# A three-phase transformer kernel on one core: the loop of phase B written out, a division and a scale step moved in phase A, weight rounding and half of the output products moved in phase B, and the residual add split between ScalarE and GpSimd

## What is computed

```python
x = x + attn_a(layernorm(x))     # 1024 tokens x 512, 32 heads of 16, full softmax, biases
x = x + ffn(layernorm(x))        # base product + routed low-rank experts, top 2 of 8
x = x + attn_b(layernorm(x))     # 32 heads of 128, 8 key/value groups
x = x + ffn(layernorm(x))        # the same weights again

def attn_b(h):                   # 4-bit weights with a scale for each 128 rows
    w = (qw - 8) * repeat(scales, 128)
    q, k, v = h @ w_q, h @ w_k, h @ w_v;  q, k = rope(q), rope(k)
    p = softmax(where(causal, q @ k.T / sqrt(128), min))
    return (p @ v) @ w_o
```

## Time and profile before

| | |
|---|---|
| median of 3 runs | 1618.2 us (1615.97 to 1626.73) |
| the profiled execution | 1621.11 us, of it 1619.3 us span |
| TensorE busy | 1480.0 us (91%) |
| VectorE busy | 1239.5 us (77%) |
| ScalarE busy | 868.7 us (54%) |
| GpSimd busy | 237.6 us (15%) |
| chain that ended last | PE 71%, DVE 12%, issue 6%, ACT 4%, DMA 4% |

### The profile page before, as it was taken

How to read it: one execution, slowest core, us unless ns; L and a number is a source line. 1 busy time by engine, 2 the same in 40 slices (tenths; PEclk the granted TensorE clock), 3 DMA queues, 4 the chain that set the end, 5 groups by cost and what they waited for, 6 DMA issues and landing times.

```text
span 1619.3 us, 25526 instructions
## 1 busy us (share of the span) xinstructions
PE 1480.0 (91%) x7932; PEld 700.4 (43%) x7932; DVE 1239.5 (77%) x2583; ACT 868.7 (54%) x1468; POOL 237.6 (15%) x174
## 2 busy tenths in 40 slices
PE   5789999999998998899998988998988999999979
PEld 3412323233332354455554544554544544555534
DVE  4288888888886378787897877897877886877863
ACT  2205767666766423565565554674654664655631
POOL 2102000000000042211212211212212221211020
PEclk8958999999999999899999999999999999999999
DMA  3993000000000323467576566675675674653631
GB/s 94 153 141 120 1 1 0 0 0 0 0 0 0 72 79 104 98 131 144 124 136 132 125 119 129 135 142 117 127 134 115 130 156 98 136 103 63 104 66 52
DMA packets 352266, 144.96 MB, mean 90 GB/s; under 512 B 314680, under 2 KB 324408, under 8 KB 352128
## 3 DMA queue, kind: packets, MB, share of 16 engines
q1 hardware_dynamic: 352144, 143.48, 42.9%
HBM read 59.64 MB, written 6.19 MB: 41 GB/s over the span
## 4 chain that ended last, share of the span: by engine, by line
PE 71%; DVE 12%; issue 6%; ACT 4%; DMA 4%; SPq 2%; ACTq 0%; DVEq 0%; POOL 0%
PE ps L1444 9%; PE ps L1446 9%; PE ps L1445 9%; PE ps L1226 9%; PE ps L1279 7%; PE ps L1265 6%; PE ps L1406 3%; PE ps L1525 3%; PE ps L1527 3%; PE ps L1526 3%; DMA hlT<-hl 2%; DVE mx L834 2%; SPq L470 2%; PE ps L1369 2%; DMA scratch<-pieces 2%
## 5 line engine op out<-in xcount | busy, mean ns | idle before, releaser
L834 DVE TENSOR_REDUCE mx<-ps 128x1 f32<-128x512 f32 x512 | 327.7, 686 | 66.6 <-PE ps L1226 64.4
L683 ACT ACTIVATE x<-ps,nmb,factor 128x128 f32<-128x128 f32 (+7 forms) x256 | 211.7, 832 | 304.3 <-DVE nmb L1034 304.3
L592 ACT ACTIVATE proj<-ps 128x1024 f32<-128x1024 f32 x256 | 248.5, 1021 | 121.6 <-PE ps L1265 120.7
L1226 PE MATMUL ps<-ks,qs 96*128 (+1 forms) x512 | 199.7, 413 | 30.9 <-DVE pieces L859 15.1
L1049 DVE SCALAR_TENSOR_TENSOR hl<-x,rden,hl 128x128 f16<-128x128 f32 (+7 forms) x256 | 208.1, 813 | 14.7 <-issue 10.8
L691 ACT ACTIVATE hl<-x,rden 128x128 f16<-128x128 f32 (+7 forms) x256 | 184.1, 767 | 27.0 <-DVE rden L1045 26.3
L1032 DVE TENSOR_REDUCE nmr<-ps 128x1 f32<-128x128 f32 (+7 forms) x256 | 191.5, 748 | 0.0
L511 POOL TENSOR_TENSOR tmp<-tmp 128x640 f32<-128x640 f32 x64 | 98.5, 1539 | 554.7 <-DVE tmp L1028 554.7
L1444 PE MATMUL ps<-wh,xTh 128*128 128x256 f16 (+1 forms) x512 | 168.5, 329 | 1.7 <-issue 1.7
L1445 PE MATMUL ps<-wl,xTh 128*128 128x256 f16 (+1 forms) x512 | 168.3, 329 | 0.0
L1446 PE MATMUL ps<-wh,xTl 128*128 128x256 f16 (+1 forms) x512 | 168.2, 329 | 0.0
(11 more groups left out here) (155 smaller groups left out, 2150.5 us busy)
## 6 DMA issues: line engine op xcount, KB each, us to landing
scale<-sp_n SPq DMA_DIRECT2D x32, 384.0 KB, 4.2
st<-in_L_attn_b_qw_q_dram SPq DMA_DIRECT2D x32, 256.0 KB, 2.6
st<-in_L_attn_b_qw_o_dram SPq DMA_DIRECT2D x32, 256.0 KB, 2.8
scale<-so_n SPq DMA_DIRECT2D x32, 256.0 KB, 3.4
qs<-scratch SPq DMA_DIRECT2D x24, 256.0 KB, 8.3
hlT<-hl SPq DMA_TRANSPOSE x256, 3.4
scratch<-pieces SPq DMA_DIRECT2D x5, 768.0 KB, 13.0
xnat<-attn_a_hidden_state_dram SPq DMA_DIRECT2D x8, 256.0 KB, 5.2
```

The lines of the kernel that those rows point to most:

```text
L592: nc.scalar.activation(pbuf[:, e % 4, :].rearrange("p (b n) -> p b n", b=2), ps[:, b:b + 2, :], ACT.Exp, scale=float(HD) ** -0.5).then_inc ...
L683: nc.scalar.activation(pr[:, h, 0:n], flat(2 * (h % 2), n), ACT.Exp, bias=nmb[:, h:h + 1], scale=factor[:, par, 0:1], accum_out=den[:, h:h ...
L834: nc.vector.tensor_reduce(mx[:, f, k // 2, k % 2:k % 2 + 1], ps[:, bank(k), :], AX.X, ALU.max).then_inc(s_mx, 1)
L1226: mm(ps[:, bank, :], qs[0:STACK, ds(g * R + h, 1), f * HALF + qt * P:f * HALF + (qt + 1) * P], ks[0:STACK, ds(g, 1), kh * HALF:(kh + 1) * ...
```

## The change

Five edits go together. (1) Phase B's hardware loop is gone, all 64 steps are written out. (2) In phase A VectorE's division comes after four maxima, not six; in the last group `normalise_scales` comes behind the division. (3) In phase B the rounding of a weight chunk on ScalarE (`high_part`) goes from between `high(1)` and `turned` to the end of the step; `PREPARED` gives step 2 two chunks (2 and 3) and step 7 none. (4) `output_second` stands behind `turn_b` in steps 0 to 3 of a group. (5) VectorE's `add` is replaced by an eviction on ScalarE (`evict`, PSUM times factor to SBUF) after the four exponentials, and a GpSimd add (`residual`) between `rope_add` and `low_part`; TensorE's next output products wait for the eviction.

```diff
+PREPARED = ((0,), (1,), (2, 3), (4,), (5,), (6,), (7,), ())
-            for t in range(T - 1):
-                step(0, t, 0)
-            with eng.Fori(0, G // 2 - 1) as gg:
...
+            for g in range(G):
+                for t in range(T):
+                    step(g, t, g % 2)
@@ gpsimd, step
+                if exists(*before(g, t, 2)):
+                    residual(g * T + t - 2, before(g, t, 2)[1])
                 if not last:
-                    low_part(g + 1, t, 1 - par)
+                    for c in PREPARED[t]:
+                        low_part(g + 1, c, 1 - par)
+            def residual(v, t):
...
+                pool.wait_ge(s_eo, v + 1)
+                pool.tensor_tensor(xnat[:, t, :], attn[:, t % 2, :], xnat[:, t, :], ALU.add).then_inc(s_xo, 1)
@@ scalar
+            def evict(v, t, par):
+                if v >= 2:
+                    act.wait_ge(s_xo, v - 1)
+                act.wait_ge(s_op, v + 1)
+                nc.scalar.activation(attn[:, t % 2, :], ps[:, 4, :], ACT.Copy,
+                                     scale=factor[:, par, 1:2]).then_inc(s_eo, 1)
@@ scalar, step
                 high(0)
                 high(1)
-                if not last:
-                    high_part(g + 1, t, 1 - par)
                 if not end:
                     turned(u + 1, t2, par if t < T - 1 else 1 - par)
                 exponentials(2)
                 exponentials(3)
+                if exists(*before(g, t, 2)):
+                    evict(u - 2, before(g, t, 2)[1], par if t >= 2 else 1 - par)
                 if exists(*before(g, t, 1)):
                     context_high(*before(g, t, 1))
                 high(2)
                 high(3)
+                if not last:
+                    for c in PREPARED[t]:
+                        high_part(g + 1, c, 1 - par)
@@ vector, group_a
                     if not last:
-                        maxima(u + 2, f, 0, 6, in_ring)
-                    elif f == 0:
-                        normalise_scales()
...
+                        maxima(u + 2, f, 0, 4, in_ring)
...
                     else:
+                        if f == 0:
+                            normalise_scales()
@@ vector, step
                 if not last:
-                    dequantise(g + 1, t)
+                    for c in PREPARED[t]:
+                        dequantise(g + 1, c)
...
-                if exists(*two):
-                    add(u - 2, two[1], par if t >= 2 else 1 - par)
@@ tensor
-                    pe.wait_ge(s_xo, u)
+                    pe.wait_ge(s_eo, u)
...
-                if exists(*two):
-                    output_second(*two, par if t >= 2 else 1 - par)
+                if exists(*two) and t >= T // 2:
+                    output_second(*two, par)
                 keys(g, t, 3, par)
                 if not end:
                     turn_b(u + 1)
+                if exists(*two) and t < T // 2:
+                    output_second(*two, par if t >= 2 else 1 - par)
```

More of the change, by code:

```diff
@@ L203, in build @@
         hid, hidT = pairs(ftmp[:, at:at + 4 * P]), pairs(ftmp[:, at + 4 * P:at + 8 * P])
+        attn = ftmp[:, at:at + 2 * D].rearrange("p (b n) -> p b n", b=2)
         pick = ftmp[:, at + 8 * P:at + 8 * P + 4 * NE].rearrange("p (j a n) -> p j a n", j=2, a=2)
@@ L328, in build @@
         s_op = sem("s_op")
+        s_eo = sem("s_attn_evicted")
         s_xo = sem("s_xo")
@@ L346, in exists, with steps @@
             return not (isinstance(g, int) and g < 0)
-        def steps(step, eng):
-            for t in range(T - 1):
-                step(0, t, 0)
-            with eng.Fori(0, G // 2 - 1) as gg:
-                for g, t in [(0, T - 1)] + [(1, t) for t in range(T)] + [(2, t) for t in range(T - 1)]:
-                    step(gg * 2 + g, t, g % 2)
-            for g, t in [(G - 2, T - 1)] + [(G - 1, t) for t in range(T)]:
-                step(g, t, g % 2)
+        def steps(step):
+            for g in range(G):
+                for t in range(T):
+                    step(g, t, g % 2)
         block = ctx.enter_context(nc.Block())
@@ L449, in _ @@
             load_chunk(1, 0)
-            def hold(what, count):
-                if not isinstance(count, int):
-                    count = sp.to_reg(count)
-                sp.wait_ge(s_tab, 48)
-                sp.wait_ge(what, count)
             def step(g, t, par):
                 u = g * T + t
-                g2, c = (g + 1, t + 1) if t < T - 1 else (g + 2, 0)
-                if not (isinstance(g2, int) and g2 >= G):
-                    hold(s_dq, g2 * CHUNKS + c - 1)
-                    hold(s_wlp, g2 * CHUNKS + c - STAGES + 1)
-                    load_chunk(g2, c)
+                g1, t1 = after(g, t)
+                if g1 + 1 < G:
+                    for c in PREPARED[t1]:
+                        sp.wait_ge(s_dq, (g1 + 1) * CHUNKS + c - 1)
+                        sp.wait_ge(s_wlp, (g1 + 1) * CHUNKS + c - STAGES + 1)
+                        load_chunk(g1 + 1, c)
                 for h in range(R):
-                    hold(s_lo, u * R + h + 1)
+                    sp.wait_ge(s_lo, u * R + h + 1)
                     if h == 0 and exists(*before(g, t, 2)):
-                        hold(s_pvb, u - 1)
+                        sp.wait_ge(s_pvb, u - 1)
                     sp.dma_start_transpose(hlT[t % 2][:, h, 0:2 * (t + 1), :],
                                            hl[:, h, 0:2 * (t + 1) * P]).then_inc(s_tp[h], 16)
-            steps(step, sp)
+            steps(step)
             for t in range(T):
@@ L531, in _ @@
             rope_add(0)
-            steps(step, pool)
+            steps(step)
+            residual(G * T - 2, T - 2)
+            residual(G * T - 1, T - 1)
             add_base_bias(xnat, 3, bb)
@@ L714, in _ @@
             tokens(2, 6, 7)
-            steps(step, act)
+            steps(step)
             root(3, 0)
+            evict(G * T - 2, T - 2, (G - 1) % 2)
             context_high(G - 1, T - 1)
             tokens(3, 0, 1, 2, 3)
+            evict(G * T - 1, T - 1, (G - 1) % 2)
             root(3, 1)
@@ L885, in group_a @@
                     if not last:
-                        maxima(u + 2, f, 6, MM, in_ring)
+                        maxima(u + 2, f, 4, MM, in_ring)
                     else:
+                        if f == 0:
+                            normalise_scales()
                         for n in (range(KC - 1), range(KC, KC + 3))[f]:
@@ L1060, in turned @@
                                                ALU.mult, ALU.subtract).then_inc(s_ql, 1)
-            def add(v, t, par):
-                dve.wait_ge(s_op, v + 1)
-                if isinstance(v, int) and v < T:
-                    for b in (t // 2,) if t < 5 else (2, 3):
-                        dve.wait_ge(s_nat[b], 64)
-                nc.vector.scalar_tensor_tensor(xnat[:, t, :], ps[:, 4, :], factor[:, par, 1:2], xnat[:, t, :],
-                                               ALU.mult, ALU.add).then_inc(s_xo, 1)
             def context_low(g, t):
@@ L1083, in step @@
                 g2, t2 = after(g, t)
-                one, two = before(g, t, 1), before(g, t, 2)
+                one = before(g, t, 1)
                 if exists(*one):
@@ L1138, in _ @@
             low_tokens(6, 7)
-            steps(step, dve)
+            steps(step)
             final_statistics(2, 3)
@@ L1144, in _ @@
             normal(3, xnat, 0, 1, 2, 3)
-            add(G * T - 2, T - 2, (G - 1) % 2)
-            final_statistics(4, 5, 6)
             context_low(G - 1, T - 1)
-            add(G * T - 1, T - 1, (G - 1) % 2)
-            final_statistics(7)
+            final_statistics(4, 5, 6, 7)
             scales(3, 1)
@@ L1555, in _ @@
             tokens(2, 6, 7)
-            steps(step, pe)
+            steps(step)
             output_first(G - 1, T - 2, (G - 1) % 2)
```

5 lines of the change are left out of this document (4 added, 1 removed).

## The result

The changed kernel takes 1632.8 us (median of 11 runs, 1629.2 to 1635.3), the kernel before 1616.0 in as many: a ratio of 1.010, 95% interval 1.008 to 1.012. It is slower by 1%, where 1617 us, a hair faster, was forecast. The profiled executions have spans of 1630.4 and 1619.3 us.

What follows compares the result with a forecast made beforehand. TensorE was taken to bound the kernel nearly everywhere, with a loop through the engines setting steps 1 to 3 of phase B. Terms summed to -1.7 us: 1619.4 profiled, 1616.5 on the median, say 1617; range 1590 to 1640.

Steps and rivals of the forecast that it cites:

- the clock: Phase A, last group: work behind the division wait, run at granted 0.50, would run at 2.4 GHz; -1.8 us.
- Phase A: Division after four maxima -15.1 us, scales behind the division -7.1, half clock behind that wait -1.8.
- The loop: Phase B's loop written out: two back edges gone, -10.2 us, and register waits gone, -2 us.
- Back edges: Phase B, step 7 ending on the loop's back edge: two of them at 5.1 us each, -10.2 us.
- registers: Phase B, looped steps 1 to 3: waits counted from a register cost 0.18 us; 3 us at most, taken as -2.
- Rounding and `output_second`: Phase B steps 0 to 3: `low_part` shuts out `low` and `dequantise`, `output_second` moves; +27 us, last group +1.5.
- The residual add: Phase B steps 5 to 7: GpSimd's add can collide with `invert`, +3 us; at the end another +3 us.
- the clock as a rival: Phase B steps 2 and 3: idle gaps each halve the clock; 14 gaps cost 24 us, 1641 us; chance 0.23.
- only `dequantise` is shut out: Phase B: `low` is not shut out beside `low_part`; 17 us less, about 1599 us; chance 0.20.
- nothing reaches the step time: Phase B: collisions merge with existing waits or engines take turns more luckily; 27 us less, about 1589; chance 0.17.

Runs made afterwards that it cites:

- a_and_loop: The kernel before with the phase A edits and the written-out loop, nothing else: 1570.2 us against 1613.8, ratio 0.975; run twice more, 1569.2 and 1569.5 us.
- second_back: The changed kernel with `output_second` back ahead of the fourth head's keys in all steps: 1598.2 us against 1614.0 for the kernel before, ratio 0.990.
- late_low: a_and_loop with the rounding at the end of the step, one chunk a step, and `low_part` one step later behind `rope_add`: 1578.2 us, ratio 0.978.
- loop_filler: a_and_loop with products that nobody reads where TensorE idles longest: 1571.7 us against 1569.2 for a_and_loop on the same chip.

## Why the prediction went wrong, point by point

In short: the step that failed is the clock. The sum has -1.8 us for it and no term for phase B, and the runs show some +20. The idle time came out as forecast in total, in part by luck. The terms in order:

**Phase A, forecast -24.0, measured -27.3.** Right step by step: the 22.2 us of waits went. The half clock was under-read: I took 3.70 us at 0.50, but the stretch went on to 518 us and lost 3.4 us, not 1.8, and one stretch of 1.7 us ahead of phase B went too.

**The loop, forecast -12.2, measured -18 alone.** Back edges 9.8 (forecast 10.2) and registers 2.8 (taken 2). What was missing is that steps 0 idle less in the written-out loop (some 3 us), and some 4.6 us of half clock, whose cause stays open.

**Rounding and `output_second`, forecast +27 and +1.5.** The step times came out as worked: steps 1, 2 and 3 at -0.27, +1.52 and +2.15 us against -0.2, +1.4 and +2.2, steps 4 to 7 at nothing, and `low` was shut out, which no row of before had shown. But I gave nearly all of it to the collision of the late rounding's `low_part`, and that was wrong: alone, the rounding makes 0.76 and 1.58 us of it. With the rounding back, 1.3 us of step 3's idle time stayed, made by `output_second` and the residual add. And `output_second` alone costs 16 us: 8 us of idle time and 8 us of half clock.

**The residual add, forecast +3 in the steps and +3 at the end, measured +35 alone.** This step failed outright too. I asked what the add would collide with, and looked for `invert`. I did not ask what is queued behind it. It waits up to 7 us for the eviction, and `low_part` stands behind it. In the changed kernel steps 4 to 7 do not show it, since there the late rounding holds `low_part` anyway: that they came out at nothing, as forecast, is luck as far as this term goes. The single edits cost 16, 12 and 35 us, some 64 in all, and together 60. That the two are so close is chance as well: what is hidden in steps 4 to 7 (2.4 us a group) comes back in steps 2, longer by 1.68 us than in `a_and_loop` where the single edits add up to 1.0, and in half clock, 24 us more loss in phase B than in `a_and_loop` where the single edits add up to 17. At the end idle time rose by 2.9 us, as forecast, and half clock made it 6.4.

**The clock, forecast -1.8 in the sum, measured +12.3 between the two profiles, and some +20 on the medians.** This term decided the sign. The 12.3 us are counted from 100 us on; the profile that the prediction started from has some 9 us more half-clock loss than the median run of its kernel, and hides that much. By idle time alone the working was good: idle time rose by 21.5 us in phase B and at the end, against 22.3 forecast. I had the clock as a rival, all or nothing, at 14 gaps in steps 2 and 3; there only six came. Eleven came around steps 0 (one more in a step 1): the kernel with the written-out loop alone idles 1.9 us there and has no half clock in groups 1 to 7, and `output_second`, which I had costed at 0.4 us there, made it 3.0. Back in its place (`second_back`), it leaves two stretches in steps 0 of groups 1 to 6 instead of eight. That single stretches come at such gaps was to be read from the earlier trace rows, so some of them belonged in the sum, not only in a rival.

Of the rivals, "only `dequantise` is shut out" and "nothing reaches the step time" are wrong (`low` at 1.85 us, steps at +1.5 and +2.2). The time lay within the range, and on the other side of no change.

## What to carry to other kernels

Where an instruction that waits is put into an in-order queue, first list what is queued behind it and which engine that work will now meet: here the queue order of two GpSimd instructions was worth 21 us in one kernel and 27 in another, and in the steps the add itself cost almost nothing. Idle time ahead of TensorE's work can cost twice, once as idle time and once as half clock behind it, so cost a lengthened gap with its share of half-clock stretches in the sum itself, not as a separate case. And try bundled edits one by one: two of these five gave some 43 us, and the other three took back 60.

## What the runs showed of the hardware

- A GpSimd instruction that reads SBUF holds up even a VectorE instruction of 2 columns with one tensor input: 1.46 us instead of 0.17 (`late_low`, L1053). The Trainium skill ("SBUF — State Buffer", section "SBUF: two separate sides") counts VectorE's 2-port modes among what is shut out; no run here shows which mode this instruction was in.
- A GpSimd memset of the same bytes holds up nothing: `low` 0.61 us and `dequantise` 0.68 us beside it.
- A half-clock stretch lost 1.7 us of clock each time, but taking it away did not always give it back: in `loop_filler`, 6.8 us of it taken away gave 3.2.
- Products that nobody reads, put into idle time, kept the clock at 1.00 in all steps but the first two of phase B and made the changed kernel 21 us faster.
